# Graph layer and expert FFN on one core: every transfer of node rows issued as two, 112 partitions and 13

## The chip, the cores and the metric

The kernel runs on one core of one Trainium2 chip, as one program. The metric is the device time of one execution in microseconds. Three runs of the kernel before gave 4287.17, 4288.52 and 4293.08 us; the median is 4288.52. The profile is of one further execution, of 4295.77 us.

## The reference, cut to what matters

There are 50,000 nodes with 256 float32 features, x, and 50,000 edges (src, dst), sorted by dst before they are passed in. Two residual layers follow each other.

```python
edge_index = jnp.stack([src, dst])          # targets, then neighbours
x = x + gnn(layernorm(x), W1, b1, W2, b2, edge_index)
x = x + ffn(layernorm(x), ...)

def gnn(x, W1, b1, W2, b2, edge_index):
    agg = segment_sum(x[nbr], dst, num_segments=n)
    cnt = segment_sum(ones, dst, num_segments=n)
    mean = agg / maximum(cnt, 1)[:, None]
    return x @ W1.T + b1 + mean @ W2.T + b2
```

The FFN adds a shared three-layer MLP (256 to 256 to 128 to 256, relu) and, of four experts (256 to 128 to 64 to 256), the two with the highest gate, weighted by a softmax of their gates.

## The kernel before, in words

The nodes are cut into 100 groups of 500 (GN, NG). A group lies in SBUF as 125 partitions (SP_) of 4 consecutive nodes (NS), so 4096 consecutive bytes of HBM per partition; the views x_v, y_v, z_v and out_v (lines 97 to 100) say so. Matrix products are made in float32r with each operand split into a high and a low part (xT_hi, xT_lo, w12_hl), three products for one.

**First stage** (block at line 211, lines 211 to 698). For every group g: x is loaded into one of four buffers (`load_x`, line 214, issue at 219); VectorE takes layernorm statistics (`stats`, 301, lines 310 to 317); POOL raises the variance to the power -0.5 (`rstd`, line 269); VectorE makes the bias (324); ScalarE writes the normalized xn (560); TensorE transposes it (620); ScalarE and VectorE copy it out as high and low part (569, 333); TensorE multiplies each quarter of 125 nodes by the two weight matrices (`rows_of`, 636 and 640), y with the bias into banks 2 and 3, z into banks 4 and 5; VectorE adds x to y and writes it to ys in two halves (`y_half`, 341); ScalarE copies z to zs in two halves (`z_half`, 575). ys and zs have two buffers each. SP stores both to HBM (252 and 256).

Beside this the edges are sorted into a table of 640 slots per group. TensorE and VectorE count the edges per group in the groups g below 16 (G_TOT; 348, 651, five onehots a group); in group 16 VectorE runs a long chain of steps (491 to 520); in groups 17 to 56 two ranking steps per group compute each edge's slot (348, 379, 387, 665, 667, 582). From group 20 on (G_SCAT) POOL scatters the edges into tab_d by indirect DMA, five per group, 400 in all (279). Before the first groups SP fills the table with a default, ten transfers on 128 partitions (235), and only then, in its own order, issues the bias row (238) and the weights of the second stage (239 to 249).

SP's order in the loop over the groups (lines 250 to 256): wait for both halves of ys, issue the y store; wait until x buffer g % 4 is free (lines 216 to 218) and issue the load of group g + 4; wait for both halves of zs, issue the z store. At the end SP waits for all stores (257 to 259). VectorE's order in one group: low parts of g + 1, bias of g + 2, sorting steps, first y half, statistics of g + 3, sorting steps, second y half. POOL's: the power for g + 3, then the five scatters.

**Second stage** (block at line 1369). Per group: POOL gathers 5 x 128 rows of z_d by the table (1325) and builds the edge onehots (1336); TensorE sums the edges into the nodes (964, 966); VectorE divides and adds y (1200); then layernorm, gate and FFN on all engines (983, 954, 1034, 1047); VectorE adds the result into x1_sb (1284). SP loads the table (1294), loads y (`load_y`, 1299) and stores out (`step_sync`, 1316); waits on these are at 1193, 1195 and 1387. The work of one group is spread over a software pipeline, and a loop with registers runs over four groups at a time.

A completion increments the transfer's semaphore by 16.

Of the kernel before, what the change touches and what calls it, by code (L numbers as in the profile page):

```python
# [18 lines left out]
NG = N // GN  # L19
SP_ = 125  # L20
# [20 lines left out]
U = 4  # L41
DX = D + 2
FILL = 800
NFILL = NROW * ROW // (P * FILL)
L1_BANKS = (0, 1, 4, 5, 0, 1)
S_ORDER = (2, 3, 0, 1)
# [13 lines left out]
def build(nc, x, src, dst, w1t, w2t, b12, wl1, bl1, wl2, bl2, wl3, b3, gw, gb,  # L60
          ident, bases16, upper16, iota16, iota, selg, tie, out, y_d, z_d, tab_d, tabx_d,
          agg_x, cnt_x):
    with ExitStack() as ctx:
# [41 lines left out]
        with ExitStack() as c1:  # L105
# [9 lines left out]
            with ExitStack() as c0:  # L115
# [95 lines left out]
                with nc.Block() as block:  # L211
                    @block.sync
                    def _(sp):
                        def load_x(g):
                            if g >= 4:
                                sp.wait_ge(a_y, 2 * (g - 4) + 2)
                                sp.wait_ge(a_stats, NS * (g - 4) + NS)
                                sp.wait_ge(a_xn, NS * (g - 4) + NS)
                            sp.dma_start(xs[:, g % 4], x_v[g]).then_inc(s_x[g % 4], 16)
                        sp.dma_start(ei[:, 0], src).then_inc(s_src, 16)  # L220
# [29 lines left out]
                        for g in range(NG):  # L250
                            sp.wait_ge(a_y, 2 * g + 2)
                            sp.dma_start(y_v[g], ys[:, g % 2]).then_inc(s_y[g % 2], 16)
                            if g + 4 < NG:
                                load_x(g + 4)
                            sp.wait_ge(a_z, 2 * g + 2)
                            sp.dma_start(z_v[g], zs[:, g % 2]).then_inc(s_z[g % 2], 16)
                        for h in range(2):
                            sp.wait_ge(s_y[h], 16 * (NG // 2))
                            sp.wait_ge(s_z[h], 16 * (NG // 2))

# [35 lines left out]
                    def _(dve):  # L296
# [7 lines left out]
                        def stats(g):  # L304
                            dve.wait_ge(s_x[g % 4], 16 * (g // 4 + 1))
                            if g >= 4:
# [30 lines left out]
                        def y_half(g, j):  # L337
                            dve.wait_ge(a_yz, NS * g + 2 * j + 2)
                            if g >= 2:
                                dve.wait_ge(s_y[g % 2], 16 * (g // 2))  # L340
                            dve.tensor_tensor(ys[:, g % 2, 2 * j:2 * j + 2, :],  # L341
# [212 lines left out]
                    def _(act):  # L554
# [16 lines left out]
                        def z_half(g, j):  # L571
                            act.wait_ge(a_yz, NS * g + 2 * j + 2)
                            if g >= 2:
                                act.wait_ge(s_z[g % 2], 16 * (g // 2))
                            act.copy(zs[:, g % 2, 2 * j:2 * j + 2, :],  # L575
                                     bank[4 + j][0:SP_, :].rearrange("p (s d) -> p s d", s=2))\
                               .then_inc(a_z, 1)
# [279 lines left out]
        with ExitStack() as c2:  # L857
# [320 lines left out]
            def graph_vector(dve, g, more):  # L1178
# [13 lines left out]
                dve.reciprocal(inv_deg[:], deg[:]).then_inc(S["inv_ready"], 1)  # L1192
                dve.wait_ge(s_yl[g.h], g.half(16))
                if g.c >= U:
                    dve.wait_ge(s_store[g.u], (g + -U).quarter(16))
                wait_alone(dve, S["inv_ready"], g.n(1, 1))
# [99 lines left out]
            def load_y(sp, g):  # L1296
                if g.c >= 2:
                    wait_alone(sp, S["x1_ready"], (g + -2).n(NS, NS))
                sp.dma_start(y_sb[g.h][:], g.of(y_v)).then_inc(s_yl[g.h], 16)

# [8 lines left out]
            def step_sync(sp, i, more):  # L1309
# [4 lines left out]
                if i.exists():  # L1314
                    wait_alone(sp, S["out_ready"], i.n(2, 2))
                    sp.dma_start(i.of(out_v), x1_sb[i.u][:]).then_inc(s_store[i.u], 16)
                if (i + 5).exists():
# [51 lines left out]
            with nc.Block() as block:  # L1369
                @block.sync  # L1370
                def _(sp):
                    def program(more):
# [13 lines left out]
                        for h in range(U):  # L1386
                            sp.wait_ge(s_store[h], 16 * (NG // U))
                    either(sp, program)
# [114 lines left out]
```

## Time and profile before

| what | value |
|---|---|
| median of 3 runs | 4288.52 us |
| profiled execution | 4295.77 us, span 4294.2 us |
| busy: PE, PEld, DVE, ACT, POOL | 3542.1, 3207.5, 2572.8, 1854.2, 2128.6 us |
| mean granted TensorE clock | 0.915 |
| DMA over the span | 324.80 MB, mean 76 GB/s |
| queue of SP | 267.28 MB, 17.9% of 16 engines |
| queue of POOL | 54.95 MB, 6.8% of 16 engines |

The span is the time from the first to the last instruction of the core. PE is TensorE's matmuls, PEld its weight loads, DVE VectorE, ACT ScalarE, POOL GpSimd, SP SyncE, which issues the transfers. PEclk is the granted TensorE clock as a share of 2.4 GHz. The DMA share is the mean busy share of the core's sixteen DMA engines in a stretch. An idle time is put down to what ended it. Names carry no buffer numbers: xs is any of its four buffers, acc any PSUM bank.

### The profile page before, as it was taken

What the parts mean: (1) busy time and instruction counts of PE and PEld (TensorE: products, weight loads), DVE (VectorE), ACT (ScalarE), POOL (GpSimd) and SP (SyncE); (2) the same over time, 40 slices, a digit from 0 to 9 for tenths busy, and PEclk for the clock granted to TensorE, in tenths of its full rate; (3) what the DMA queues carried; (4) which work ended last, traced back from release to release, by engine and by line L of the source; (5) the groups of instructions that cost most, each with busy time, mean ns of one, the idle gap of its engine ahead of it and who ended that gap; (6) DMA issues with size and microseconds to landing.
All of it is one profiled execution on the core that took longest, in us unless ns stands there. A gap on an engine that the chain in (4) does not pass through costs nothing.

```text
span 4294.2 us, 71441 instructions
## 1 busy us (share of the span) xinstructions
PE 3542.1 (82%) x22640; PEld 3207.5 (75%) x22640; DVE 2572.8 (60%) x7146; ACT 1854.2 (43%) x3285; POOL 2128.6 (50%) x1604
## 2 busy tenths in 40 slices
PE   5766665665556564999999999999999999999998
PEld 4665555555555563988888888888888888888897
DVE  5554444443222223777777777777777777777775
ACT  2332332332222221555555555555555555555554
POOL 0003444444444455655555655555555555555561
PEclk9887788777777776999999999999999999999999
DMA  4323333333333332211111111111111111111110
GB/s 145 108 102 93 92 95 94 91 92 102 100 103 102 103 105 62 68 62 60 61 61 59 61 62 63 60 60 61 61 59 60 63 63 62 59 61 61 60 63 25
DMA packets 120631, 324.80 MB, mean 76 GB/s; under 512 B 40370, under 2 KB 43662, under 8 KB 120389
## 3 DMA queue, kind: packets, MB, share of 16 engines
q1 hardware_dynamic: 83588, 267.28, 17.9%
q0 software_dynamic: 36800, 54.95, 6.8%
q8 instruction: 72, 1.18, 0.1%
q14 instruction: 171, 1.39, 0.1%
HBM read 175.10 MB, written 160.90 MB: 78 GB/s over the span
## 4 chain that ended last, share of the span: by engine, by line
PE 51%; issue 5%; DVE 3%; ACT 2%; POOL 1%; DVEq 0%; DMA 0%; ACTq 0%; POOLq 0%
PE acc L983 15%; PE acc L954 9%; PE acc L1034 8%; PE acc L964 6%; PE acc L966 5%; PE acc L1047 3%; PE acc L1007 2%; PE acc L999 1%; ACT h1f L1069 1%; PE acc L1030 1%; PE acc L993 1%; POOL e_oh L1336 0%; DVE x_sb L1284 0%; DVE x_sb L1200 0%; ACT h_hi L1076 0%
## 5 line engine op out<-in xcount | busy, mean ns | idle before, releaser
L1336 POOL TENSOR_SCALAR e_oh<-iota_sb,tab 128x500 fp32r<-128x500 f32 x500 | 762.8, 1536 | 438.9 <-PE acc L966 438.8
L1325 POOL DMA_INDIRECT rows<-z_d,tab x500 | 593.5, 1187 | 634.1 <-issue 577.5
L983 PE MATMUL acc<-x1T_hi,wl_hl 128*128 128x500 f32 x2400 | 680.4, 395 | 12.4 <-ACT h1f L1069 10.1
L640 PE MATMUL acc<-w_hl,xT_hi 128*125 128x256 f32 x3200 | 684.4, 325 | 0.0
L310 DVE BATCH_NORM_STATS2 a_st<-xs 125x6 f32<-125x256 f32 x400 | 140.5, 414 | 892.1 <-DMA xs<-in_x 892.1
L640 PEld LDWEIGHTS acc<-w_hl,xT_hi 128*125 128x125 f32 x3200 | 583.0, 234 | 3.6
L575 ACT COPY zs<-acc 125x512 f32<-125x512 f32 x200 | 117.2, 586 | 1079.6 <-DMA z_d<-zs 779.3
L269 POOL TENSOR_TENSOR a_rstd<-a_var,half_neg 125x4 f32<-125x4 f32 x100 | 120.9, 1209 | 895.5 <-DVE a_var L317 895.5
L279 POOL DMA_INDIRECT tab_d<-pair,idx x400 | 481.1, 1203 | 117.4 <-issue 115.9
L964 PE MATMUL acc<-e_hi,e_oh 128*125 128x258 f32 x2000 | 484.7, 284 | 55.8 <-POOL e_oh L1336 55.8
L983 PEld LDWEIGHTS acc<-x1T_hi,wl_hl 128*128 128x128 f32 x2400 | 439.6, 189 | 116.5 <-ACT h1f L1069 25.0
L966 PE MATMUL acc<-e_lo,e_oh 128*125 128x256 f32 x2000 | 484.1, 282 | 0.0
L1034 PE MATMUL acc<-wl_hl,h_hi 128*125 128x256 f32 x2400 | 480.6, 282 | 0.0
L1227 DVE TENSOR_TENSOR h_lo<-h1f,h_hi 128x500 fp32r<-128x500 f32 x600 | 396.8, 675 | 52.1 <-ACT h_hi L1076 49.3
L964 PEld LDWEIGHTS acc<-e_hi,e_oh 128*125 128x125 f32 x2000 | 375.1, 188 | 59.8 <-issue 55.9
L1069 ACT ACTIVATE h1f<-acc,bl_sb 128x500 f32<-128x500 f32 x600 | 405.7, 676 | 14.1 <-PE acc L983 6.3
L636 PE MATMUL acc<-bias_r,two_ones 128*125 128x256 f32 x400 | 174.2, 435 | 271.7 <-DVE ys L341 269.5
L1034 PEld LDWEIGHTS acc<-wl_hl,h_hi 128*125 128x125 f32 x2400 | 394.9, 187 | 0.0
L954 PE MATMUL acc<-h_hi,wl_hl 128*128 128x500 f32 x1200 | 386.1, 403 | 6.8 <-ACT h1f L1069 6.7
L640 PE MATMUL acc<-w_hl,xT_lo 128*125 128x256 f32 x1600 | 379.6, 325 | 0.0
L966 PEld LDWEIGHTS acc<-e_lo,e_oh 128*125 128x125 f32 x2000 | 374.9, 187 | 4.3
L1076 ACT CAST h_hi<-h1f 128x500 fp32r<-128x500 f32 x600 | 365.6, 609 | 17.6
(141 smaller groups left out, 6996.1 us busy)
## 6 DMA issues: line engine op xcount, KB each, us to landing
xs<-in_x SPq DMA_DIRECT2D x100, 500.0 KB
y_d<-ys SPq DMA_DIRECT2D x100, 500.0 KB
z_d<-zs SPq DMA_DIRECT2D x100, 500.0 KB
y_sb<-y_d SPq DMA_DIRECT2D x100, 500.0 KB
out<-x_sb SPq DMA_DIRECT2D x100, 500.0 KB
rows<-z_d,tab POOLq DMA_INDIRECT x500
tab_d<-pair,idx POOLq DMA_INDIRECT x400
tab_d<-fill SPq DMA_DIRECT2D x10, 400.0 KB, 7.0
```

What stands on the lines that cost most here:

```text
L279: pool.indirect_dma_start(out=tab_d, out_offset=bass.IndirectOffsetOnAxis(ap=idx[:, n:n + 1], axis=0), in_=pair[:, 2 * n:2 * n + ROW], in_ ...
L640: mm = pe.matmul(o, (xT_hi, xT_lo)[a][:, g % 2, f, cols_], w12_hl[:, w, f, wt], start=b == 4 and n == 0, stop=n == 5)
L954: mm = pe.matmul(bank[t % 2][:, 0:GN], wl2_hl[:, w, 2 * t + e, :], (h1_hi, h1_lo)[a][:, 2 * t + e, :], start=n == 0, stop=n == 5)
L964: pe.matmul(bank[2 + s][0:SP_, 0:DX], e_oh[:, q, cols_], e_hi[:, q, :], start=q == 0, stop=False)
L966: mm = pe.matmul(bank[2 + s][0:SP_, 0:D], e_oh[:, q, cols_], e_lo[:, q, :], start=False, stop=q == EQ - 1)
L983: mm = pe.matmul(bank[L1_BANKS[t]][:, 0:GN], wl1_hl[:, w, f, t * P:(t + 1) * P], (x1T_hi, x1T_lo)[a][:, f, :], start=n == 0, stop=n == 5)
L1034: mm = pe.matmul(o, (h2_hi, h2_lo)[a][:, t, cols_], wl3_hl[:, w, t, :], start=False, stop=n == 3 * H2T - 1)
L1069: act.activation(h1f[t % NF1][:], bank[L1_BANKS[t]][:, 0:GN], ACT.Relu, bias=bl1_sb[:, t:t + 1]).then_inc(S["h1_relu_ready"], 1)
L1076: act.copy(h1_hi[:, t, :], h1f[t % NF1][:]).then_inc(S["h1_hi_ready"], 1)
L1227: dve.tensor_tensor(h1_lo[:, t, :], h1f[t % NF1][:], h1_hi[:, t, :].bitcast(F32), ALU.subtract).then_inc(S["h1_lo_ready"], 1)
L1325: pool.indirect_dma_start(out=rows[g.h][:, q, :], out_offset=None, in_=z_d, in_offset=bass.IndirectOffsetOnAxis(ap=tab[g.h][:, q * ROW:q * ...
L1336: pool.tensor_scalar(e_oh[:, q, :], iota_sb[:], tab[g.h][:, q * ROW + 1:q * ROW + 2].bitcast(F32), None, ALU.is_equal).then_inc(S["e_oh_re ...
```

## The change

Each of the five kinds of transfer of node rows (x in, y out, z out, y in, out) is issued as two: partitions 0 to 111 and partitions 112 to 124. Both increment the same semaphore, so each wait for such a transfer counts 32 per group where it counted 16.

```diff
--- before.py
+++ after.py
@@ -42,6 +42,8 @@
 DX = D + 2
 FILL = 800
 NFILL = NROW * ROW // (P * FILL)
+SPLIT = (slice(0, 112), slice(112, SP_))
+LOAD = 16 * len(SPLIT)
 L1_BANKS = (0, 1, 4, 5, 0, 1)
 S_ORDER = (2, 3, 0, 1)
 PARTS = ((0, 0), (1, 0), (0, 1))
@@ -216,7 +218,8 @@
                                 sp.wait_ge(a_y, 2 * (g - 4) + 2)
                                 sp.wait_ge(a_stats, NS * (g - 4) + NS)
                                 sp.wait_ge(a_xn, NS * (g - 4) + NS)
-                            sp.dma_start(xs[:, g % 4], x_v[g]).then_inc(s_x[g % 4], 16)
+                            for r in SPLIT:
+                                sp.dma_start(xs[r, g % 4], x_v[g][r]).then_inc(s_x[g % 4], 16)
                         sp.dma_start(ei[:, 0], src).then_inc(s_src, 16)
                         sp.dma_start(io16[:], iota16).then_inc(s_c0, 16)
                         load_x(0)
@@ -249,14 +252,16 @@
                         sp.dma_start(tie_sb[:], tie).then_inc(s_cst, 16)
                         for g in range(NG):
                             sp.wait_ge(a_y, 2 * g + 2)
-                            sp.dma_start(y_v[g], ys[:, g % 2]).then_inc(s_y[g % 2], 16)
+                            for r in SPLIT:
+                                sp.dma_start(y_v[g][r], ys[r, g % 2]).then_inc(s_y[g % 2], 16)
                             if g + 4 < NG:
                                 load_x(g + 4)
                             sp.wait_ge(a_z, 2 * g + 2)
-                            sp.dma_start(z_v[g], zs[:, g % 2]).then_inc(s_z[g % 2], 16)
+                            for r in SPLIT:
+                                sp.dma_start(z_v[g][r], zs[r, g % 2]).then_inc(s_z[g % 2], 16)
                         for h in range(2):
-                            sp.wait_ge(s_y[h], 16 * (NG // 2))
-                            sp.wait_ge(s_z[h], 16 * (NG // 2))
+                            sp.wait_ge(s_y[h], LOAD * (NG // 2))
+                            sp.wait_ge(s_z[h], LOAD * (NG // 2))
 
                     @block.gpsimd
                     def _(pool):
@@ -302,7 +307,7 @@
                             dve.wait_ge(s_c, count[0])
 
                         def stats(g):
-                            dve.wait_ge(s_x[g % 4], 16 * (g // 4 + 1))
+                            dve.wait_ge(s_x[g % 4], LOAD * (g // 4 + 1))
                             if g >= 4:
                                 dve.wait_ge(a_rs, g - 3)
                                 dve.wait_ge(a_nbr, g - 3)
@@ -337,7 +342,7 @@
                         def y_half(g, j):
                             dve.wait_ge(a_yz, NS * g + 2 * j + 2)
                             if g >= 2:
-                                dve.wait_ge(s_y[g % 2], 16 * (g // 2))
+                                dve.wait_ge(s_y[g % 2], LOAD * (g // 2))
                             dve.tensor_tensor(ys[:, g % 2, 2 * j:2 * j + 2, :],
                                               bank[2 + j][0:SP_, :]
                                               .rearrange("p (s d) -> p s d", s=2),
@@ -571,7 +576,7 @@
                         def z_half(g, j):
                             act.wait_ge(a_yz, NS * g + 2 * j + 2)
                             if g >= 2:
-                                act.wait_ge(s_z[g % 2], 16 * (g // 2))
+                                act.wait_ge(s_z[g % 2], LOAD * (g // 2))
                             act.copy(zs[:, g % 2, 2 * j:2 * j + 2, :],
                                      bank[4 + j][0:SP_, :].rearrange("p (s d) -> p s d", s=2))\
                                .then_inc(a_z, 1)
@@ -1190,9 +1195,9 @@
                                   ALU.max).then_inc(S["deg_ready"], 1)
                 dve.wait_ge(S["deg_ready"], g.n(1, 1))
                 dve.reciprocal(inv_deg[:], deg[:]).then_inc(S["inv_ready"], 1)
-                dve.wait_ge(s_yl[g.h], g.half(16))
+                dve.wait_ge(s_yl[g.h], g.half(LOAD))
                 if g.c >= U:
-                    dve.wait_ge(s_store[g.u], (g + -U).quarter(16))
+                    dve.wait_ge(s_store[g.u], (g + -U).quarter(LOAD))
                 wait_alone(dve, S["inv_ready"], g.n(1, 1))
                 if more:
                     wait_alone(dve, s_agf, g.n(NS, NS))
@@ -1296,7 +1301,8 @@
             def load_y(sp, g):
                 if g.c >= 2:
                     wait_alone(sp, S["x1_ready"], (g + -2).n(NS, NS))
-                sp.dma_start(y_sb[g.h][:], g.of(y_v)).then_inc(s_yl[g.h], 16)
+                for r in SPLIT:
+                    sp.dma_start(y_sb[g.h][r], g.of(y_v)[r]).then_inc(s_yl[g.h], 16)
 
             def load_more(sp, g):
                 if g.c:
@@ -1313,7 +1319,8 @@
                     load_y(sp, i + 4)
                 if i.exists():
                     wait_alone(sp, S["out_ready"], i.n(2, 2))
-                    sp.dma_start(i.of(out_v), x1_sb[i.u][:]).then_inc(s_store[i.u], 16)
+                    for r in SPLIT:
+                        sp.dma_start(i.of(out_v)[r], x1_sb[i.u][r]).then_inc(s_store[i.u], 16)
                 if (i + 5).exists():
                     load_table(sp, i + 5)
 
@@ -1384,7 +1391,7 @@
                             step_sync(e, i, more)
                         steps(run, sp)
                         for h in range(U):
-                            sp.wait_ge(s_store[h], 16 * (NG // U))
+                            sp.wait_ge(s_store[h], LOAD * (NG // U))
                     either(sp, program)
 
                 @block.gpsimd
```

## Rows read from the trace of the kernel before

**Rows 1.** Stretches: length, busy us (x instructions) of each engine, PEclk, DMA share, GB/s.

```profile
36.70:256.70 220.00, 156.88 (x1041) 149.69 (x1042) 118.24 (x312) 65.28 (x127) 15.12 (x15) 0.87 0.30 104
...
299.60:957.00 657.40, 408.24 (x2468) 366.69 (x2466) 305.19 (x804) 204.80 (x383) 270.06 (x218) 0.79 0.34 93
957.00:1604.30 647.30, 386.92 (x2538) 378.40 (x2538) 187.91 (x600) 172.94 (x333) 300.77 (x254) 0.77 0.37 102
...
1740.00:4260.00 2520.00, 2474.39 (x15907) 2208.78 (x15905) 1852.95 (x5137) 1342.62 (x2326) 1455.01 (x1046) 1.00 0.19 60
```

**Rows 2.** Waits, whole span: who waited for whom, us in total, times, longest.

```profile
DVE a_st L310 <- DMA xs<-in_x: 892.1, 95, 11.8
ACT zs L575 <- DMA z_d<-zs: 779.3, 82, 11.0
```

**Rows 3.** DMA issues by line: the x load, KB of one.

```profile
xs<-in_x SPq DMA_DIRECT2D x100, 500.0 KB
```

**Rows 4.** Stretches of the start and of one early group, columns as in rows 1.

```profile
14.00:30.00 16.00, 1.90 (x8) 1.54 (x8) 10.43 (x39) 5.80 (x11) 3.55 (x3) 1.00 0.95 362
62.19:76.42 14.23, 10.44 (x65) 9.93 (x65) 7.34 (x20) 4.10 (x8) 1.02 (x2) 0.77 0.31 109
```

**Rows 5.** Timeline, one ranking group: start us, us, engine, line, operation, [idle before].

```profile
807.49 0.27 SPq L252 DMA_DIRECT2D y_d<-ys  x1
...
820.02 1.08 DVE L310 BATCH_NORM_STATS2 a_st<-xs 125x6 f32<-125x256 f32 x3 [8.97 <-DMA xs<-in_x]
...
824.29 0.27 SPq L252 DMA_DIRECT2D y_d<-ys  x1
```

**Rows 6.** Timeline, the first two groups.

```profile
47.03 1.02 PE L620 MATMUL acc<-ident_sb,xn 125*128 125x125 f32 x8
...
47.95 0.30 SPq L252 DMA_DIRECT2D y_d<-ys  x1
...
48.70 0.41 SPq L256 DMA_DIRECT2D z_d<-zs  x1
...
55.63 1.02 PE L620 MATMUL acc<-ident_sb,xn 125*128 125x125 f32 x8
...
59.68 0.43 DVE L310 BATCH_NORM_STATS2 a_st<-xs 125x6 f32<-125x256 f32 x1 [6.47 <-DMA xs<-in_x]
```

**Rows 7.** Timeline, late groups without ranking.

```profile
1551.96 1.40 DVE L310 BATCH_NORM_STATS2 a_st<-xs 125x6 f32<-125x256 f32 x4 [10.80 <-DMA xs<-in_x]
...
1553.93 1.04 POOL L269 TENSOR_TENSOR a_rstd<-a_var,half_neg 125x4 f32<-125x4 f32 x1 [6.61 <-DVE a_var L317]
...
1554.48 0.27 SPq L252 DMA_DIRECT2D y_d<-ys  x1
...
1561.26 1.19 POOL L279 DMA_INDIRECT tab_d<-pair,idx  x1 [0.30 <-issue]
...
1593.41 0.28 PE L636 MATMUL acc<-bias_r,two_ones 128*125 128x256 f32 x1
...
1594.94 0.28 PE L636 MATMUL acc<-bias_r,two_ones 128*125 128x256 f32 x1
```

**Rows 8.** Timeline, VectorE in group 16: the y halves around its chain.

```profile
261.57 0.69 DVE L341 TENSOR_TENSOR ys<-acc,xs 125x512 f32<-125x512 f32 x1
...
278.80 0.69 DVE L341 TENSOR_TENSOR ys<-acc,xs 125x512 f32<-125x512 f32 x1
```

**Rows 9.** Timeline, the ends of the stages.

```profile
36.69 0.65 PE L620 MATMUL acc<-ident_sb,xn 125*128 125x125 f32 x2 [8.84 <-DMA bias_r<-st_bl]
...
1614.32 1.19 POOL L279 DMA_INDIRECT tab_d<-pair,idx  x1 [0.30 <-issue]
1635.02 1.12 DVE L1404 MEMSET rows<- 128x1280 f32 x1 [25.34 <-PEq L716]
...
4283.83 0.26 SPq L1316 DMA_DIRECT2D out<-x_sb  x1
```

## The prediction

> **What bounds the kernel now.** I read four views. The stretches first [rows 1]: from 36.7 to 1604.3 us (the first stage, 100 groups) no engine is near its limit. TensorE is busy 408.24 of 657.40 us in the middle of it, at a granted clock of 0.79 of 2.4 GHz, while the sixteen DMA engines together show a share of 0.30 to 0.37. In the second stage (1740 to 4260 us) TensorE is busy 2474.39 of 2520.00 us at clock 1.00 and the DMA share is 0.19. So the stages have different limits, and only the first can gain much from faster transfers.
>
> The waits second [rows 2]: VectorE sits idle for 892.1 us ahead of the statistics of a fresh x group, ScalarE for 779.3 us ahead of the copy into zs, which must wait for an earlier z store. Both wait for the queue of SP.
>
> The transfer third [rows 3, 4]: each load or store of a group is 500.0 KB (512,000 bytes) on 125 partitions, 4096 bytes on each. In the stretch from 62.19 to 76.42 us, where only those run, the share is 0.31: 5 engines of 16 (0.3125), moving 109 GB/s, or 22 GB/s each. In 14 to 30 us, where loads and fills of 128 partitions stand in the queue, the share is 0.95 and 362 GB/s move: 15.2 engines at 23.8 GB/s each. A 125-partition transfer thus uses five full engines and leaves eleven idle. The Trainium skill, "DMA: Bandwidth & Descriptors", section on why a DMA increments its semaphore by 16, says that the number of engines is the largest up to 16 that divides the outermost size, so 5 for 125; the share of 0.31 agrees.
>
> The order of time last [rows 5]: y of one group is issued at 807.49, x for four groups on right behind it; VectorE can start on that x at 820.02, and the next y is issued at 824.29. That is a loop: 12.53 us until x is usable, then 4.27 us of VectorE (statistics, one onehot, one select, one sum, the second y half), 16.80 us in all. The z store is issued in the same loop and fills the queue in the 4.27 us: three transfers of 4.65 us on five engines are 14 us, and the first groups take just that, 14.23 us [rows 4]. Transfers are the first stage's bound.
>
> **The change, part by part.** (a) The 112-partition piece. Nearest rows: 125 partitions run on 5 engines, 128 on about 16 [rows 4]. Bounds: 5 and 16 engines. I take 16, as 112 is a multiple of 16 as 128 is, and 125 is five times 25. Then each engine gets 7 rows of 4096 bytes. (b) The 13-partition piece: 13 rows, between one engine (13 rows on it) and 13 (one row each). I take 13. The fullest engine then has 8 rows, 32,768 bytes, at 22 GB/s 1.5 us for a whole transfer, against 4.65 us. (c) Twice as many issues on SP: one costs 0.27 to 0.41 us [rows 5, 6], so y and x take about 1.4 us to issue where they took 0.7. They run beside the first piece's transfer and SP has time (it waits in every group for ys), so I add 0.4 us at most to the landing of x, nothing elsewhere. (d) The larger semaphore counts move nothing.
>
> The fixed part of a landing comes from the first, empty queue [rows 6]: y issued at 47.95, x behind it, VectorE starts at 59.68: 11.73 us, of which two transfers at 4.65 are 9.3, so 2.4 us are left. New time from y's issue to usable x: 2.4 + 2 x 1.5 = 5.4 us. Bounds: 5.0 us, and 8 us if the issues, the table's scatters (on the same engines) or an uneven engine delay the last piece.
>
> What is late next, by kind of group:
> - Groups 0 to 15. The loop is 5.4 + 2.5 (statistics and y half) = 7.9 us. TensorE is slower: two starts of a group's transposes at clock 1.00, with transfers not yet in the way, are 47.03 and 55.63, 8.6 us apart [rows 6]. I take 8.7.
> - Group 16 has the long chain on VectorE: y halves at 261.57 and 278.80, 17.2 us apart [rows 8], and it hardly waits for x. Stays.
> - Groups 17 to 56 (ranking): 5.4 + 4.27 = 9.7 us, and 0.2 to 0.4 where POOL scatters; I take 9.9 for three groups and 10.1 for 37. VectorE's own work is below it: 305.19 us busy in 657.40 [rows 1] at 16.8 us per group is 7.8 us.
> - Groups 57 to 99: the loop is 5.4 + 2.52 = 7.9 us [rows 7]. POOL takes over: one power at 1553.93 and five scatters, the fifth starting at 1561.26 and 1.19 + 0.30 us long, are 8.8 us per group. POOL's power for a group feeds the next norm, so it paces all. I take 8.85 and 5 us once for the splitting of the second stage's weights. TensorE needs less: a quarter of its rows is 1.53 us (1593.41 to 1594.94), four are 6.1, with transposes 7.0 us.
>
> Before the first group, TensorE waits 8.84 us at 36.69 for the bias row [rows 9], a small transfer behind the fills and the five engines' four x loads (four times 102 KB on each of those engines, which become 33 KB: 69 KB x 4 at 22 GB/s is 12.5 us less). I let the stage start 9.5 us earlier; bounds 0 and 12.
>
> Sum, by the issue of y: group 0 at 47.95 - 9.5 = 38.5; group 15 at 38.5 + 15 x 8.7 = 169; group 16 at 186; group 19 at 216; group 56 at 216 + 37 x 10.1 = 590; POOL's last scatter 43 x 8.85 + 5 later, at 976. Today the second stage's first memset is at 1635.02, 20.7 us after POOL's last scatter started, because y and z stores of the last group were still landing on five engines [rows 9]; with those short, I take 4 us: 980. So 655 us go. (e) In the second stage the y loads and the stores of out are hidden behind a TensorE that is full; I cost them at nothing. If that cover were gone, they would show as idle time of VectorE ahead of x_sb. Only the last store is bare: issued at 4283.83, and the span ends at 4294.2; 3 us less.
>
> 4294.2 - 655 - 3 = 3636 us of span, 3638 with the 1.6 us that lie around it (4295.77 in all). The profiled run stands 7 us above the median of 4288.52, so I forecast 3630 us. A measurement of this kernel can tell about 0.2%, 9 us, from no change.
>
> A rule speaks against all this. What the rows show is that one 125-partition transfer leaves eleven engines idle [rows 4]. The Trainium skill, same page, "Rules for kernel authors", says of two transfers to disjoint partition halves not to bother, since both halves spray over all sixteen engines and share them. By it nothing would be gained; it speaks of halves that already use sixteen, which the 0.31 here denies.
>
> **The rivals.**
> 1. TensorE stays at its lower clock. It was idle some 5 us at a stretch in every group and the clock averaged 0.77 to 0.79 [rows 1]; now it would be idle about 2 us. If it stayed there, its own work per group would be 408.24 / 657.40 x 16.8 = 10.4 us in the ranking groups and 386.92 / 647.30 x 15.9 = 9.5 us later: 0.3 x 37 + 0.65 x 43 = 39 us more, 3670. Against it: at 8.6 us per group and full work the clock was 1.00.
> 2. x lands late (8 us): the loop is 10.5, 12.7 and 10.5 us. 1.8 x 16 + 2.6 x 40 + 1.65 x 43 = 204 us more, 3834. For it: the scatters' packets stand on any engine, and the last of sixteen counts. Against: the rate per engine was no lower with sixteen busy than with five.
> 3. The 13-row piece stands on one engine: it then has 20 rows per transfer, 3.7 us; usable x after 2.4 + 7.4 = 9.8 us, loops of 12.3, 14.2 and 12.3 us: 3.6 x 16 + 4.1 x 40 + 3.5 x 43 = 372 us more, 4000. No row shows a transfer of 13 partitions.
> 4. The pieces stay on the same five engines, by whatever chooses them; then it is slower. 112 rows give 23 to the fullest and 13 give 3, together 26 for 25: in a queue that is full, each transfer costs 0.19 us more, three per group 0.57, times 100 is 57 us: 4345. It decides as soon as the pieces use no more than five engines. The rule against halves, taken literally, gives this case or no change.
> 5. The change does not do what it says, in that y, x and z land faster but another wait of the same length stands behind (ScalarE's or POOL's). The trace names none; no change, 4289.
>
> **How the numbers follow.** Forecast 0.60 (its own range 3590 to 3700), rival 1 0.10, rival 2 0.13, rival 3 0.10, rival 4 0.03, rival 5 0.02; 0.02 for still faster than 3590. The range goes from 3580, where the ranking groups reach POOL's pace of 8.9 us (1.2 x 40 = 48 us less), to 3840, which takes in rivals 1 and 2. Faster 0.95, same 0.02, slower 0.03.
>
> **What would show it.** In the changed profile: y's issues 8.5 to 9 us apart in groups 0 to 15, about 10 from 17 to 56 and 8.9 after; idle time of VectorE ahead of a_st from 892 to under 150 us; ScalarE's wait for z_d stores gone; POOL's idle time ahead of a_rstd near nothing after group 57; the clock above 0.9 in the first stage; the second stage still some 2655 us long. GB/s in the first stage near 170. A share of 0.31 with y's issues still 14 to 17 us apart would make rival 4 true. A second stage longer by over 10 us would say that its transfers were not hidden or that shorter bursts disturb it.

## The result, and the profile after

The changed kernel takes 3662.79 us (median of 3661.92, 3662.26, 3663.32 and 3840.89), the kernel before 4290.8 us (median of four runs, 4287.17 to 4293.43). The run of 3840.89 us was a slow one, at a mean granted clock of 0.84 where the others had 0.98, and ratios and intervals here leave such runs out. The ratio is 0.8536, with an interval of 0.8519 to 0.8553: 628 us less. The profiled execution took 3661.92 us, its span 3660.4.

Stretches of the changed kernel: length, busy us (x instructions) of TensorE, its weight loads, VectorE, ScalarE, POOL, then PEclk, DMA share, GB/s.

```profile
39.80:177.00 137.20, 125.40 (x984) 119.66 (x983) 112.36 (x304) 62.37 (x122) 14.48 (x15) 1.00 0.54 169
...
227.70:638.80 411.10, 329.41 (x2305) 297.68 (x2305) 289.75 (x763) 194.22 (x360) 261.79 (x212) 0.93 0.51 140
638.80:1043.00 404.20, 339.32 (x2598) 324.44 (x2598) 191.89 (x608) 184.28 (x343) 304.55 (x258) 0.95 0.60 170
1140.00:3626.00 2486.00, 2477.59 (x16033) 2231.82 (x16032) 1868.56 (x5188) 1355.59 (x2350) 1446.95 (x1057) 1.00 0.20 62
```

Against [rows 1]: the share of the DMA engines was 0.30 to 0.37 and is now 0.51 to 0.60, the rate was 93 to 104 GB/s and is 140 to 170, and TensorE is busy 80 to 91% of these stretches of the first stage, where it was 60 to 71%. The second stage is full as before.

Waits of the changed kernel: who waited for whom, us in total, times, longest.

```profile
DVE a_st L315 <- DMA xs<-in_x: 350.4, 95, 5.4
POOL a_rstd L274 <- DVE a_var L322: 336.1, 99, 16.4
...
ACT zs L580 <- DMA z_d<-zs: 126.0, 45, 4.1
...
DVE z L1139 <- issue: 49.8, 21, 2.6
```

The two waits of [rows 2] shrink from 892.1 to 350.4 us and from 779.3 to 126.0 us, but the first still comes 95 times: x still arrives late in nearly every group. The last row is one that I had not looked at; before it reads as follows.

```profile
DVE z L1134 <- issue: 103.4, 21, 5.3
```

One ranking group and one late group in the changed kernel's timeline (start us, us, engine, line, operation, [idle before]).

```profile
480.02 0.77 SPq L256 DMA_DIRECT2D y_d<-ys  x2
...
481.19 1.03 SPq L222 DMA_DIRECT2D xs<-in_x  x2
482.28 0.81 SPq L261 DMA_DIRECT2D z_d<-zs  x2
...
486.98 1.41 DVE L315 BATCH_NORM_STATS2 a_st<-xs 125x6 f32<-125x256 f32 x4 [2.52 <-DMA xs<-in_x]
...
491.25 0.77 SPq L256 DMA_DIRECT2D y_d<-ys  x2
...
860.25 0.77 SPq L256 DMA_DIRECT2D y_d<-ys  x2
...
866.93 1.41 DVE L315 BATCH_NORM_STATS2 a_st<-xs 125x6 f32<-125x256 f32 x4 [4.87 <-DMA xs<-in_x]
...
869.45 0.77 SPq L256 DMA_DIRECT2D y_d<-ys  x2
```

It is the loop of [rows 5], shorter: y issued at 480.02, x usable 6.96 us later (12.53 before), 4.27 us of VectorE as before, 11.23 us in all (16.80 before). Late it is 6.68 and 2.52, 9.20 us.

The time by stage: the first y is issued at 39.84 (47.95 before), groups 0 to 15 are 9.15 us apart (14.3), group 16 takes 17.2 as before, groups 20 to 56 take 11.4 each (17.1), and the late ones up to group 96 take 9.4 (15.6). These are the distances of the y stores' issues: group 19 is issued at 227.65, group 56 at 650.55. The rows at the end of the first stage and of the run:

```profile
1042.95 0.77 SPq L256 DMA_DIRECT2D y_d<-ys  x2
...
1054.67 1.19 POOL L284 DMA_INDIRECT tab_d<-pair,idx  x1 [0.30 <-issue]
1061.33 1.12 DVE L1411 MEMSET rows<- 128x1280 f32 x1 [17.73 <-PEq L721]
...
3653.86 0.93 SPq L1323 DMA_DIRECT2D out<-x_sb  x2
```

From 1635.02 [rows 9] to 1061.33 the first stage has lost 573.7 us. From the memset to the end of the span were 2659.2 us; now they are 2599.1, another 60.1 us. These two are the whole difference of the spans, 633.8 us.

How many engines a transfer uses can be read from the packets of SP's queue (queue, kind: packets, MB, share of 16 engines), before and after:

```profile
q1 hardware_dynamic: 83588, 267.28, 17.9%
```

```profile
q1 hardware_dynamic: 95588, 267.33, 23.8%
```

The changed kernel has 12,000 packets more, and the packets under 512 B grow by as many (40,370 to 52,369). That is 24 for each of the 500 transfers: one small packet for each engine that takes part makes 16 + 13 = 29 of them where the whole transfer had 5.

### The profile page after: what moved, and what is told of

Read it like the earlier page. It is cut to its first block, busy times and chain, and to the rows that moved or that the text cites. A ratio compares the mean times of both kernels' runs of the same rounds, so it can differ in the third digit from the quotient of the medians.

```text
span 3660.4 us, 72293 instructions
## 1 busy us (share of the span) xinstructions
PE 3387.8 (93%) x22640; PEld 3079.8 (84%) x22640; DVE 2570.7 (70%) x7146; ACT 1861.7 (51%) x3285; POOL 2103.8 (57%) x1604
## 2 busy tenths in 40 slices
DMA packets 132633, 324.88 MB, mean 89 GB/s; under 512 B 52369, under 2 KB 55661, under 8 KB 132388
## 4 chain that ended last, share of the span: by engine, by line
PE 65%; issue 2%; ACT 1%; DVE 1%; POOL 1%; DVEq 0%; DMA 0%; ACTq 0%; POOLq 0%
PE acc L988 20%; PE acc L959 11%; PE acc L1039 11%; PE acc L969 7%; PE acc L971 6%; PE acc L1052 4%; PE acc L1012 2%; PE acc L1004 1%; PE acc L1035 1%; ACT h1f L1074 1%; PE acc L998 1%; POOL e_oh L1343 0%; POOL rows L1332 0%; ACT h_hi L1081 0%; DVE x_sb L1289 0%
## 5 line engine op out<-in xcount | busy, mean ns | idle before, releaser
L1332 POOL DMA_INDIRECT rows<-z_d,tab x500 | 570.0, 1140 | 280.2 <-issue 258.8
L988 PE MATMUL acc<-x1T_hi,wl_hl 128*128 128x500 f32 x2400 | 665.9, 392 | 0.0
L645 PE MATMUL acc<-w_hl,xT_hi 128*125 128x256 f32 x3200 | 599.6, 293 | 0.0
L645 PEld LDWEIGHTS acc<-w_hl,xT_hi 128*125 128x125 f32 x3200 | 493.5, 199 | 2.5
L315 DVE BATCH_NORM_STATS2 a_st<-xs 125x6 f32<-125x256 f32 x400 | 140.5, 414 | 350.4 <-DMA xs<-in_x 350.4
L988 PE MATMUL acc<-x1T_lo,wl_hl 128*128 128x500 f32 x1200 | 367.5, 388 | 0.0
L1101 ACT ACTIVATE ga<-z 125x16 f32<-125x16 f32 x100 | 21.6, 216 | 649.9 <-DVE z L1145 649.9
L1039 PE MATMUL acc<-wl_hl,h_lo 128*125 128x256 f32 x1200 | 337.5, 281 | 0.0
L645 PE MATMUL acc<-w_hl,xT_lo 128*125 128x256 f32 x1600 | 335.7, 293 | 0.0
```

The lines of the kernel that those rows point to most:

```text
L645: mm = pe.matmul(o, (xT_hi, xT_lo)[a][:, g % 2, f, cols_], w12_hl[:, w, f, wt], start=b == 4 and n == 0, stop=n == 5)
L988: mm = pe.matmul(bank[L1_BANKS[t]][:, 0:GN], wl1_hl[:, w, f, t * P:(t + 1) * P], (x1T_hi, x1T_lo)[a][:, f, :], start=n == 0, stop=n == 5)
L1039: mm = pe.matmul(o, (h2_hi, h2_lo)[a][:, t, cols_], wl3_hl[:, w, t, :], start=False, stop=n == 3 * H2T - 1)
L1332: pool.indirect_dma_start(out=rows[g.h][:, q, :], out_offset=None, in_=z_d, in_offset=bass.IndirectOffsetOnAxis(ap=tab[g.h][:, q * ROW:q * ...
```

## The experiments

Three questions: is it the number of engines or the halving as such; what sets the loop, the rate or the place of x in the queue; and where do the 60 us of the second stage come from.

**1 and 2. The stages apart.** Experiment 1 is the changed kernel with the second stage's transfers whole again:

```diff
-                for r in SPLIT:
-                    sp.dma_start(y_sb[g.h][r], g.of(y_v)[r]).then_inc(s_yl[g.h], 16)
+                sp.dma_start(y_sb[g.h][:], g.of(y_v)).then_inc(s_yl[g.h], 16)
...
-                    for r in SPLIT:
-                        sp.dma_start(i.of(out_v)[r], x1_sb[i.u][r]).then_inc(s_store[i.u], 16)
+                    sp.dma_start(i.of(out_v), x1_sb[i.u][:]).then_inc(s_store[i.u], 16)
```

> Only the first stage's transfers (x in, y out, z out) are split; the second stage's y load and out store are whole. The changed kernel's second stage was 60 us shorter (2599 against 2659 us), which I had costed at nothing. Theory A: those 60 us belong to the second stage's own transfers, whose five engines delay VectorE's return to the start of its loop (idle 4.9 us before the gate logits once per four groups, 2.3 in the changed kernel). Then this kernel has the changed kernel's first stage and the old second one: 3720 us, idle 4.9 us in 21 returns. Rival B: the second stage is shorter through something that the first leaves behind; then 3662 us.

Experiment 2 is the kernel before with these two places split and nothing else.

> Only the second stage's y load and out store are split; the first stage is the old one. Theory A: about 4290 less 60 us, 4230 us, with VectorE's idle time at the 21 loop returns at 2.3 us instead of 4.9. Rival B: no change, 4290 us.

Measured: 3726.35 us (ratio 0.8688, 0.8673 to 0.8702) and 4231.15 us (0.9862, 0.9845 to 0.9878). The savings of 0.131 and 0.014 make 0.145, against the change's 0.146: the stages add up. From the second stage's memset to the end are 2656.0 us in experiment 1 (1065.3 to 3721.3) and 2598.2 in experiment 2 (1631.8 to 4230.0), and one wait goes with them. Experiment 1:

```profile
DVE z L1139 <- issue: 103.8, 21, 5.3
```

Experiment 2:

```profile
DVE z L1136 <- issue: 50.6, 21, 2.6
```

**10 and 11. The two transfers of the second stage apart**, each alone split in the kernel before: y's load in 10, out's store in 11.

> The kernel before with only the second stage's y load split. It is issued 3 us ahead of VectorE's return to the start of its loop, and whole it holds the five low engines for 4 to 5 us. Theory: it is this load that delays the return; then the 21 returns are 2.3 us long here and 60 us go, 4230 us, as with both split. Rival: the out store, issued at the very return, delays it; then 4290 us.

> The kernel before with only the second stage's out store split. The mirror of the run with y alone: by the theory that the y load delays VectorE's return to the start of its loop nothing changes but the last store's landing, 4285 to 4290 us and returns of 4.9 us; by the rival 4230 us.

Measured: 4230.82 us (0.9868, 0.9851 to 0.9884) with the wait at 50.1 us, and 4285.3 us (0.9991, 0.9982 to 1.0001) with it at 103.0. So the load of y alone carries the gain. The waiting stands where VectorE goes back to the start of its loop, once in four groups. In the kernel before:

```profile
1996.24 0.26 SPq L1299 DMA_DIRECT2D y_sb<-y_d  x1
1999.38 0.29 SPq L1316 DMA_DIRECT2D out<-x_sb  x1
...
2003.98 0.19 DVE L1134 TENSOR_REDUCE z<-acc 125x16 f32<-125x32 f32 x1 [4.85 <-issue]
2004.23 0.30 PEld L983 LDWEIGHTS acc<-x1T_hi,wl_hl 128*128 128x128 f32 x2 [0.43 <-DVE z L1134]
```

In the changed kernel:

```profile
1927.64 0.84 SPq L1305 DMA_DIRECT2D y_sb<-y_d  x2
1930.79 0.86 SPq L1323 DMA_DIRECT2D out<-x_sb  x2
1932.81 0.19 DVE L1139 TENSOR_REDUCE z<-acc 125x16 f32<-125x32 f32 x1 [2.27 <-issue]
```

The profile names nothing that VectorE waits for, for 4.85 us with a y load on five engines issued shortly before it and for 2.27 us with a load on sixteen; the next weight load of TensorE waits for z. A loop of four groups takes 104.2 us before and 101.7 now. That the load's form sets the wait is shown by 10 and 11.

What VectorE waits for is in the trace's packets, which the rows above leave out. Each of the 21 waits holds exactly one packet of the queue of kind "instruction", of 8192 bytes, and VectorE goes on 1.9 to 2.2 us after that packet starts. Before the change the packet starts 2.7 to 3.4 us into the wait, within 0.3 us of the end of the y load on the last of its five engines; in the changed kernel it starts after 0.4 to 0.7 us. Experiment 10 shows the short time and experiment 11 the long one. So the wait is a fetch of instructions, and the 2.5 us that went are its delay behind the load. In experiment 7 below, 29 rows of the load stand on one engine and land after VectorE is back, and the fetch is early all the same (0.4 to 0.7 us). The fetch is thus not held by the load as such; that it needs one of the five engines, and not the one with the 29 rows, fits all these runs, but the packets don't name their engines, so this is argued.

**3. The same two pieces, but 115 and 10**, in the changed kernel:

```diff
-SPLIT = (slice(0, 112), slice(112, SP_))
+SPLIT = (slice(0, 115), slice(115, SP_))
```

> All five transfers in two pieces as in the changed kernel, but 115 and 10 partitions. Theory width: what counts is the number of engines, and by the Trainium skill (DMA: Bandwidth & Descriptors, why a DMA increments its semaphore by 16) 115 partitions run on 5 engines and 10 on 10, so the fullest engine has 24 rows instead of 25: first stage 4% shorter at most, 4230 to 4320 us in all, DMA share near 0.32 in the early groups. Rival pieces: two issues run beside each other and that alone gives the gain; then near 3660 us.

Measured: 4217.54 us (0.9831, 0.9811 to 0.985). The stretch from 62 to 140 us, columns as above:

```profile
62.00:140.00 78.00, 55.99 (x381) 53.42 (x382) 43.79 (x115) 24.60 (x48) 5.63 (x6) 0.87 0.35 112
```

The y stores of the early groups are 13.7 us apart, about 14.23 x 24 / 25. Two pieces on five engines bring 74 of the 628 us; 115 stays on five engines (23 rows each), 10 rows add one row to ten engines. The queue has 88,588 packets, 10 more per transfer than before the change: 5 + 10 engines instead of 5. The wait of the loop's return stays too (100.3 us).

**7. A small piece that doesn't divide: 96 and 29** (slices 0 to 96 and 96 on).

> All five transfers in two pieces of 96 and 29 partitions. Theory width, with the rule of the Trainium skill (DMA: Bandwidth & Descriptors, why a DMA increments its semaphore by 16): 96 partitions run on 16 engines, 6 rows each, but 29 is prime and stands on one engine, which then has 35 rows where the old five had 25. The first stage follows the fullest engine: 14.23 x 35 / 25 = 19.9 us for each early group, somewhat more in the ranking ones, 2010 us for all; 40 us or so more in the second stage: about 4760 us, slower than the kernel before, with a DMA share below 0.2 in the early groups. Rival: a prime number of partitions spreads as well as 13 did; then near 3660 us.

Measured: 4464.22 us in one run, 176 us more than the kernel before in the same session. The groups:

```profile
104.17 0.65 SPq L256 DMA_DIRECT2D y_d<-ys  x2
...
118.05 1.41 DVE L315 BATCH_NORM_STATS2 a_st<-xs 125x6 f32<-125x256 f32 x4 [7.85 <-DMA xs<-in_x]
...
120.56 0.67 SPq L256 DMA_DIRECT2D y_d<-ys  x2
```

They are 16.3 to 17.5 us apart, 16.75 in the middle. With 29 rows on one engine beside 6 of the 96, that engine has 35 rows per transfer, 105 per group, and 105 x 0.159 us = 16.7 us (0.159 us per 4096 bytes is 25.8 GB/s, from experiment 6 below). When the rows of the 96 are through, the stretch shows that one engine alone:

```profile
113.00:116.00 3.00, 3.00 (x25) 2.73 (x23) 0.00 (x0) 1.54 (x3) 0.00 (x0) 1.00 0.06 26
```

A share of 0.06 is one engine of sixteen, and it moves 26 GB/s. My expectation had the direction, and 300 us too much, because it used 22 GB/s. The return of VectorE's loop stays short here (48.9 us).

So the sizes 125, 115, 112, 13 and 29 behave as 5, 5, 16, 13 and 1 engines; the packets of this experiment agree too (89,588, which is 16 + 1 per transfer). The Trainium skill, "DMA: Bandwidth & Descriptors", section on why a DMA increments its semaphore by 16, gives the largest divisor up to 16; all of these agree.

**9. Three pieces: 96, 16 and 13**, the same rows per engine, one more issue per transfer.

> All five transfers in three pieces of 96, 16 and 13 partitions: the fullest engine has 6 + 1 + 1 = 8 rows as in the changed kernel, only the issues on SP are half as many again. Theory issue time: from y's issue to usable x the changed kernel needs 6.7 to 7.0 us, of which SP's four issues are some 2 us; two more issues ahead of the last row of x cost 2 x 0.4 = 0.8 us in the loop of every group but the 16th: 80 us more, 3740 us. Rival: SP's issues run beside the transfers and cost nothing, and the 1.4 us that the forecast of the landing missed lie in the engines; then 3663 us within 10.

Measured: 3677.49 us (0.8576, 0.8559 to 0.8593), 15 us above the change for 500 more issues, where the theory of a costly SP wanted 3740. So an issue is nearly free here (0.03 us each). That the earlier piece's transfer covers it fits, and is argued.

**8. x split, y and z whole** in the first stage.

> The changed kernel with the first stage's y and z stores whole again and only x in two pieces (the second stage as in the changed kernel). Theory: the five low engines have 25 + 25 + 8 = 58 rows a group instead of 24 and instead of 75; x waits behind y's 25: 4.65 + 1.5 + 2.4 + 0.5 = 9.1 us to usable x, so loops of 11.6 us early, 13.4 ranking, 11.6 late; 16 x 2.4 + 40 x 2.1 + 43 x 2.4 = 226 us more than the changed kernel, 3890 us. Rival: the split of x is all that matters, as only x is waited for; then near 3660 us.

Measured: 3938.58 us in one run, a_st waits 600.8 us. Two rows of an early group:

```profile
101.84 0.27 SPq L255 DMA_DIRECT2D y_d<-ys  x1
...
113.12 1.41 DVE L313 BATCH_NORM_STATS2 a_st<-xs 125x6 f32<-125x256 f32 x4 [6.52 <-DMA xs<-in_x]
```

Usable x comes 11.28 us after y's issue here, and 9.5 us on average over the groups (8.5 to 11.9), though x itself is on sixteen engines. The changed kernel has 6.8 us on average; the y store ahead of x has 17 rows more on five engines, 17 x 0.159 = 2.7 us, and that is the difference. The stores must be split as well.

**12. The kernel before, x issued ahead of y**, nothing split:

```diff
-                            sp.dma_start(y_v[g], ys[:, g % 2]).then_inc(s_y[g % 2], 16)
                             if g + 4 < NG:
                                 load_x(g + 4)
+                            sp.dma_start(y_v[g], ys[:, g % 2]).then_inc(s_y[g % 2], 16)
```

> The kernel before, nothing split, four buffers, only the x load issued ahead of the y store. After the run with five buffers on the old kernel (3953 us, early groups 11.8 us apart, 132 GB/s at a share of 0.32) the theory is: the old kernel was held by the loop through the landing of x (y's 25 rows, x's 25 rows and some 3.7 us that no row accounts for), and five engines could do 11.9 us a group. With y's 25 rows (4.0 us) behind x, x is usable after about 7.7 us, the loop is 10.2 us early and late, 12.0 ranking, at or under what five engines need, so it comes out like the one with five buffers: 3930 to 4000 us. Rival: buffers, not the place in the queue, made that gain (a load a whole group early also rides over the stores' bursts); then above 4100 us.

Measured: 3979.62 us (0.9273, 0.9193 to 0.9353). The groups, on the same five engines:

```profile
103.99 0.26 SPq L219 DMA_DIRECT2D xs<-in_x  x1
...
113.27 1.41 DVE L310 BATCH_NORM_STATS2 a_st<-xs 125x6 f32<-125x256 f32 x4 [4.56 <-DMA xs<-in_x]
...
115.83 0.26 SPq L219 DMA_DIRECT2D xs<-in_x  x1
```

11.84 us per group instead of 14.23, with the same bytes on the same engines. So five engines can carry a group in 11.8 us, and the 14.23 us of the kernel before were not their limit. Where the rest went can be seen when the group of [rows 4] is cut in pieces (columns as in rows 1):

```profile
62.80:67.30 4.50, 3.26 (x15) 3.17 (x16) 3.55 (x7) 0.00 (x0) 0.00 (x0) 0.50 0.32 83
...
69.80:76.42 6.62, 4.68 (x38) 4.34 (x36) 2.49 (x11) 1.83 (x4) 0.55 (x1) 1.00 0.33 132
```

The same five engines move 83 GB/s just after y is issued and 132 GB/s later. Packet by packet, a row of 4096 bytes takes 0.25 us on average in the first piece and 0.159 in the second, and so it is in each of the groups 1 to 14. Four of the five engines are through with the z store before at 62.35 to 62.49, y has been issued at 62.19, and their next row starts at 62.95, so the queue runs dry once in a group. In experiments 12 and 6 a row of these groups takes 0.16 us throughout. Slow rows thus go with a queue that has just run dry, and experiment 4 has them with x at the front as well; why they are slow, no run shows.

**6. The kernel before with five x buffers** (the load of group g+5 behind the y store of group g, so that nobody needs it at once):

```diff
-xs = sb("xs", [SP_, 4, NS, D], F32, c0)
+xs = sb("xs", [SP_, 5, NS, D], F32, c0)
...
-if g + 4 < NG:
-    load_x(g + 4)
+if g + 5 < NG:
+    load_x(g + 5)
```

> The kernel before with five buffers of x, nothing split. Theory full queue: three transfers of 25 rows on each of five engines take 14.2 us whatever the order, so the early groups stay at 14.2, the ranking ones fall from 16.9 towards 15 (the scatters' packets stand on the same engines), the late ones from 15.6 to about 15: near 4195 us. Rival latency: the old loop was 12.5 us of landing time of x and not the engines' load; without it the groups would take 9 to 10 us, near 3750 us.

Measured: 3952.55 us (0.9212, 0.9185 to 0.9239), between the two theories. The stretch and the waits:

```profile
62.00:140.00 78.00, 61.31 (x436) 57.27 (x434) 52.62 (x141) 25.92 (x51) 7.05 (x7) 0.93 0.32 132
```

```profile
ACT zs L576 <- DMA z_d<-zs: 641.8, 91, 9.4
...
DVE a_st L311 <- DMA xs<-in_x: 2.2, 5, 0.7
```

Now the queue stays full (ScalarE still waits for its z stores, nobody for x), and at the same share, 0.32 against 0.31, the five engines move 132 GB/s against 109 [rows 4]: 25.8 GB/s each (132 / (16 x 0.32)), one row of 4096 bytes in 0.159 us. 75 rows per group at that rate are 11.9 us, about the pace of experiment 12 (11.8). The y stores here come 8.6 to 13.1 us apart, as the fifth buffer lets the first groups run ahead. So the share is no rate: slow packets count as much as fast ones.

**4 and 5. The loop taken away from the changed kernel**: x issued ahead of y (4), or five x buffers (5). The edit of 4:

```diff
-                            for r in SPLIT:
-                                sp.dma_start(y_v[g][r], ys[r, g % 2]).then_inc(s_y[g % 2], 16)
                             if g + 4 < NG:
                                 load_x(g + 4)
+                            for r in SPLIT:
+                                sp.dma_start(y_v[g][r], ys[r, g % 2]).then_inc(s_y[g % 2], 16)
```

> The changed kernel with the x load issued ahead of the y store. The changed kernel needs 6.7 to 7.0 us from y's issue to usable x, where 5.4 were forecast. Theory order: 1.15 us of that are y's two issues on SP and 1.5 us y's rows ahead of x on every engine. Then x is usable after 4.3 us, the loop is 8.6 us in the ranking groups and 6.8 later, and TensorE (8.7), VectorE and POOL (9.2 and 8.85) are the bounds: 16 x 0.45 + 40 x 2.1 + 43 x 0.4 = 108 us less, 3555 us. Rival fixed: the landing time of x is a latency that its place in the queue does not change; then 3660 us.

> The changed kernel, y issued first as there, with five buffers of x instead of four, so that a load has a whole group more to land. Theory: in the changed kernel the landing of x closes the loop everywhere but in group 16, and nothing else does; without it the groups take what they took with x issued ahead of y (8.6 early, 8.85 ranking, 8.55 late, where POOL's power and five scatters are the bound): 3520 to 3530 us and no idle time of VectorE ahead of a_st. Rival: moving y behind x helped by something else (y's store out of the way of the next one, say); then more than 3560 us remain.

Measured: 3521.42 us (0.8207, 0.8193 to 0.8221) and 3535.2 us (0.8239, 0.8215 to 0.8263). Experiment 4 beats both kernels, by 141 us the changed one, and comes out 34 us below its expectation; experiment 5 lies 5 us above its range. Its waits and a ranking and a late stretch of its timeline:

```profile
DVE a_nb L329 <- POOL a_rstd L274: 134.5, 39, 3.7
...
DVE a_st L315 <- DMA xs<-in_x: 40.8, 41, 2.5
```

```profile
482.77 0.76 SPq L222 DMA_DIRECT2D xs<-in_x  x2
...
486.57 1.41 DVE L315 BATCH_NORM_STATS2 a_st<-xs 125x6 f32<-125x256 f32 x4 [0.27 <-DMA xs<-in_x]
...
816.29 1.07 POOL L274 TENSOR_TENSOR a_rstd<-a_var,half_neg 125x4 f32<-125x4 f32 x1
...
824.83 1.04 POOL L274 TENSOR_TENSOR a_rstd<-a_var,half_neg 125x4 f32<-125x4 f32 x1
825.91 0.16 DVE L329 SCALAR_TENSOR_TENSOR a_nb<-a_mv,a_rstd 125x4 f32<-125x4 f32 x1 [3.64 <-POOL a_rstd L274]
```

Here x is usable 3.80 us after its own issue; where VectorE waits for x at all in the ranking groups, it is 3.8 to 5.5 us, 4.4 in the middle. The wait for x falls from 350.4 to 40.8 us. The late groups run at POOL's 8.54 us (one power and five scatters, 816.29 to 824.83); the early ones take 8.6, the ranking ones 8.9. The prediction gave the change itself 8.7, 9.9 to 10.1 and 8.85.

## Why the prediction was right, and where its terms were off

The forecast was 3630 us, its range 3580 to 3840; measured were 3662.8. The mechanism of the first stage holds: the y, x and z transfers moved from 5 engines to 16 and 13, and the loop from y's issue to usable x shortened in every group. Two pieces that stay on five engines (experiment 3) give some 12% of the gain, and pieces with a bad remainder (7) a loss. But the 33 us between forecast and result hide two errors of opposite sign: the first stage was forecast 81 us too short and the second 57 us too long; without the second, which no term foresaw, the forecast would have been 90 us off, so its closeness is in part luck. The other 9 us are the prediction's last step: it took off 8 us because the profiled run of the kernel before lay above the median, and the profiled run of the changed kernel lies 0.9 us below its own.

- **Engines, terms (a) and (b): right.** 112 on 16, 13 on 13 engines, as the count of packets says.
- **SP's issues, term (c): right in size.** Up to 0.4 us was allowed, though the 5.4 us of the sum leave it out; 500 more cost 15 us in the whole run (9).
- **Usable x after 5.4 us: too short. This is the term that failed.** The groups show 6.7 to 7.0. It came from an engine's rate of 22 GB/s, read as 109 GB/s over a share of 0.31 [rows 4], and from what that left of 11.73 us as the fixed part, 2.4. The two pieces of that stretch shown at experiment 12 say that 22 GB/s was a mean of slow rows after y's issue and of rows at 25.8 GB/s. At 25.8 a whole transfer on five engines takes 25 x 0.159 = 4.0 us, and 11.73 - 2 x 4.0 leaves 3.8 us, not 2.4. Then the new loop is 3.8 + 2 x 8 x 0.159 = 6.3 us; 0.4 to 0.7 us are not accounted for. The 3.8 us are no pure latency either: the slow rows are in them, and the changed kernel has such rows too (0.23 us each on average from 94.96 to 99.40). Experiment 4 leaves less beside the rows: 3.8 to 4.4 us from x's issue to usable x, of which x's own 8 rows take 1.3. What the fixed part is made of stays open.
- **Early groups: 8.7 forecast (TensorE), 9.15 measured**, still x. 15 x 0.45 = 7 us. Ranking groups: 9.9 to 10.1 forecast, 11.1 measured for the first three and 11.4 for the 37 others: 3 + 49 us. Late groups: POOL's 8.85 forecast, 9.4 measured, as x kept POOL waiting some 0.8 us a group; from the y store of group 56 (650.55) to POOL's last scatter (1054.67) are 404 us where 386 were forecast, +18. Of the 336.1 us of idle time ahead of a_rstd only 30.2 fall into these groups, so that sign came out nearly as forecast. Start 1 us late; and the memset comes 6.7 us after the last scatter's start, where 4 were taken, +3. Together 81 us: 1061.3 against 980.
- **Second stage, term (e) at nothing: wrong.** I named idle time of VectorE ahead of x_sb as the sign to look at and only considered a loss. Of the 60.1 us, 103.4 - 49.8 = 53.6 us are VectorE's loop returns and 3.8 us the last store (10.4 us from its issue to the end of the span before, 6.5 now; a gain of 3 was forecast); 2.7 us are not accounted for. The row was in the trace of before, the releaser "issue" hid it from me, and a full TensorE at 2474.39 of 2520.00 us left 46 us in that stretch that I did not ask after.
- **"Transfers are the first stage's bound": half right.** Three transfers of 4.65 us fill 14.2 us by construction, as the 22 GB/s were read from those very 14.23 us. The bound was the landing of one x behind one y: without a byte less on any engine, the order alone gives 7% (12) and a fifth buffer 8% (6). Width matters all the same: experiment 6 against 5 differ by width alone, 3952.6 and 3535.2 us.
- **Rivals.** 1 (lower clock) did not come: PEclk 1.00, 0.93 and 0.95, against 0.87, 0.79 and 0.77 [rows 1]. 2 (x late) had the right place at half its size: x is 1.3 to 1.6 us late instead of 2.6. 3 and 4 (the small piece on one engine, or the pieces on the same five) are out for 112 and 13; one engine is what 29 shows, five are what 115 shows. 5 does not hold, but in experiment 4 the next wait is POOL's, as 5 would have it.
- **The signs.** Right were the clock above 0.9, POOL's idle time late, and nearly the 170 GB/s (140 to 170). Wrong were the distances of y's issues (9.15, 11.4 and 9.4 us for 8.5 to 9, about 10 and 8.9), the wait for x (350.4 us, not under 150), ScalarE's wait for z stores (126.0 us, not gone) and the length of the second stage (2599 us, not 2655).
- **The rule on two disjoint halves**, which the prediction weighed (the Trainium skill, "DMA: Bandwidth & Descriptors", "Rules for kernel authors"), says not to bother. Read for transfers that already use all engines it is not touched by any run here; for one that uses five, the runs go against it by 628 us.

## What to carry to other kernels

Look at the partition count of each large transfer: where it has no divisor near 16, cut it into a multiple of 16 and a small remainder, and keep the remainder's own divisors in mind (96 and 29 was worse than no cut). Before that, ask which transfer somebody waits for and issue it ahead of those that nobody waits for; here this cost no line and gave 7% on the old kernel and 4% on the new. And before taking an engine's rate from a stretch, cut the stretch in pieces: here one group held 83 and 132 GB/s at the same share, and only the second was the rate of a full queue. That an engine waits for a store is no proof of a full queue, as ScalarE did so before the change as well [rows 2]. A busy share tells how many engines hold packets, not how fast they move.

## What the runs showed of the hardware that I had not expected

The return of VectorE's loop costs 4.9 us with a five-engine load in flight and 2.3 us without, 21 times in the second stage, and of the transfers tried only the form of that one load changes it (50.1 and 103.0 us in experiments 10 and 11). The packets show it as a fetch of 8192 bytes of instructions that starts late. The DMA share of five engines was 0.31 to 0.32 at 109 and at 132 GB/s. Rows of 4096 bytes took 0.25 us where the queue had just run dry and 0.159 us in a full one. And in windows of half a microsecond sixteen engines do not hold their rate. In the changed kernel, behind a y store issued at 94.46:

```profile
94.46:94.96 0.50, 0.50 (x6) 0.50 (x6) 0.50 (x2) 0.00 (x0) 0.46 (x1) 1.00 0.00 0
94.96:95.46 0.50, 0.50 (x5) 0.35 (x3) 0.50 (x2) 0.00 (x0) 0.00 (x0) 1.00 0.47 147
...
97.00:97.50 0.50, 0.50 (x6) 0.50 (x6) 0.43 (x3) 0.00 (x0) 0.00 (x0) 1.00 0.64 188
...
98.50:99.00 0.50, 0.50 (x6) 0.49 (x5) 0.50 (x2) 0.50 (x2) 0.00 (x0) 1.00 0.49 164
...
99.50:100.00 0.50, 0.50 (x6) 0.50 (x6) 0.50 (x2) 0.50 (x2) 0.00 (x0) 1.00 0.90 328
```

Nothing moves in the first half microsecond, and the rate falls to 164 and 188 GB/s where the last row has 328. The packets show both gaps and slower rows: most of the small packets that end y's transfer fall between 96.5 and 97.2, and the rows up to 99.40 take 0.23 us on average instead of 0.159. No run closed either.
